# First attention: keys projected once and doubled by DMA. Second attention: logits as ring items, divisors moved by DMA, experts' weights split in its last batch

## The reference

```python
q = (x @ Mq).reshape(B, 8, 1024, 64)            # first attention; k alike
scores = einsum('bhqk,bhck->bhqc', q, k) / 8
att = softmax(scores, over the queries q)
out = einsum('bqhc,bhcd->bqhd', att as [B, C, H, C], v)
x = layernorm(x + out)

scores = einsum('bhst,...')                     # second: 16 heads, 4 of 8 channels, / 2
ao = softmax(scores) @ V                        # V has 4 channels a head
m = concat(ao, zeros) @ o_w + o_b
p = softmax(m @ router_w + router_b)            # 8 experts
keep the 2 largest of p, divided by their sum -> combine
moe = sum over e: combine[e] * (gelu(m @ w1[e] + b1[e]) @ w2[e] + b2[e])
x = layernorm(x + 0.3 * moe)
```

## Time and profile before

| | us |
|---|---|
| median of 3 runs | 1932.06 (1929.78 to 1940.83) |
| the profiled execution | 1930.25 |
| its span, first to last instruction | 1928.5 |
| first loads and values | 0 to 24.6 |
| first attention | 24.6 to 521.5 |
| layer norm, projections, first row maxima | 521.5 to 585.1 |
| second attention, blocks 0 to 30 | 585.1 to 1182.25 |
| its last block and its tail | 1182.25 to 1238.4 |
| routing | 1238.4 to 1263.7 |
| experts | 1263.7 to 1456.8 |
| state-space layer, sorted experts, gather | 1456.8 to 1928.5 |

### The profile page before, as it was taken

One profiled execution on the slowest core, in us unless ns is written; L12 is line 12 of the kernel. 1 busy time (PEld: TensorE's weight loads), 2 busy tenths in 40 slices (PEclk: granted clock), 3 DMA queues, 4 the chain that ended last, 5 costly groups with the idle time before them and its releaser, 6 DMA issues. The chain is left out here.

```text
span 1928.5 us, 39668 instructions
## 1 busy us (share of the span) xinstructions
PE 1630.0 (85%) x14336; PEld 901.3 (47%) x14337; DVE 1319.5 (68%) x1787; ACT 1274.3 (66%) x2303; POOL 476.2 (25%) x656
## 2 busy tenths in 40 slices
PE   5999999999979999999999999699997436704870
PEld 4555655555543443344444444377772112304860
DVE  2667677676679999999999994245554596341445
ACT  2777777777738898998989997378885760402221
POOL 0222222222162000000000000189991232042006
PEclk8999999999969999999999998599998768857995
DMA  5000000000013100110010000164300000412013
GB/s 203 2 0 0 0 0 0 0 0 0 1 36 99 28 16 2 23 24 1 16 28 5 2 1 1 44 148 97 93 17 14 1 0 0 151 34 77 23 30 84
DMA packets 42890, 62.64 MB, mean 32 GB/s; under 512 B 7768, under 2 KB 28000, under 8 KB 42016
## 3 DMA queue, kind: packets, MB, share of 16 engines
q1 hardware_dynamic: 38688, 55.97, 10.5%
q0 software_dynamic: 4096, 5.25, 1.0%
HBM read 34.85 MB, written 9.57 MB: 23 GB/s over the span
## 5 line engine op out<-in xcount | busy, mean ns | idle before, releaser
L862 ACT ACTIVATE m_probs<-m_ring 128x512 f32<-128x512 f32 x1024 | 545.8, 595 | 97.9 <-PE m_ring L776 81.5
L928 DVE TENSOR_REDUCE m_half_max<-m_pairs 128x2 f32<-128x1024 f32 x512 | 587.8, 1217 | 13.9 <-PE m_pairs L759 12.8
L351 DVE TENSOR_REDUCE a_neg_max<-a_scores 128x1 f32<-128x1024 f32 x257 | 310.5, 1215 | 118.6 <-PE a_scores L287 118.5
L341 ACT ACTIVATE a_probs<-a_scores,a_neg_max 128x1024 f32<-128x1024 f32 x256 | 285.3, 1114 | 127.2 <-DVE a_neg_max L351 127.2
L776 PE MATMUL m_ring<-m_q_max,m_k 32*128 32x512 f32 x1024 | 330.8, 505 | 5.8 <-DVE m_q_max L942 4.0
L791 PE MATMUL m_acc<-m_probs,m_v_aug 128*32 128x256 f32 (+1 forms) x4032 | 332.1, 403 | 0.0
L759 PE MATMUL m_pairs<-m_k,m_q 32*128 32x512 f32 x1024 | 263.3, 511 | 13.3 <-DVE m_half_max L928 9.6
L776 PEld LDWEIGHTS m_ring<-m_q_max,m_k 32*128 32x128 f32 x1024 | 152.4, 185 | 226.7 <-ACT m_probs L862 131.1
L287 PE MATMUL a_scores<-a_q,a_k 64*128 64x512 f32 x1032 | 257.2, 617 | 0.9 <-ACT a_probs L341 0.9
L386 POOL TENSOR_TENSOR a_scaled<-values,a_inv 128x128 f32<-128x128 f32 x256 | 102.7, 401 | 417.6 <-DVE a_inv L369 283.9
L1323 POOL TENSOR_TENSOR e_g_parts<-e_gated,e_g_parts 128x512 fp32r<-128x512 f32 x128 | 164.7, 1321 | 16.5 <-ACT e_g_parts L1269 15.6
(11 more groups left out here) (254 smaller groups left out, 1848.3 us busy)
## 6 DMA issues: line engine op xcount, KB each, us to landing
e_gates<-sorted_results SPq DMA_DIRECT2D x64, 256.0 KB, 3.7
m_k<-m_k_init SPq DMA_DIRECT2D x8, 512.0 KB, 8.8
m_q<-xT SPq DMA_DIRECT2D x8, 512.0 KB, 10.3
sorted_tokens<-xT SPq DMA_DIRECT2D x5, 512.0 KB, 6.0
f_sorted_rows<-sorted_tokens SPq DMA_DIRECT2D x10, 256.0 KB, 4.9
sorted_results<-f_out SPq DMA_DIRECT2D x10, 256.0 KB, 2.2
e_w<-e_w_dram SPq DMA_DIRECT2D x1, 2064.0 KB, 7.8
xT<-x_t_dram SPq DMA_DIRECT2D x1, 2048.0 KB, 7.6
```

Of the source, the lines that this page charges most:

```text
L341: nc.scalar.activation(probs[:, g, :], scores[:, slot(h * G + g), :], ACT.Exp, bias=neg_max[:, g:g + 1], accum_out=total[:, g:g + 1]).then ...
L351: nc.vector.tensor_reduce(neg_max[:, i % G:i % G + 1], scores[:, slot(i), :], AX, ALU.max, negate=True).then_inc(max_done, 1)
L862: nc.scalar.activation(probs[:, u % SLOTS, head, :], ring[:, bank, :], ACT.Exp, scale=0.5).then_inc(ring_taken, 1)
L928: nc.vector.tensor_reduce(half_max[:, pair // PAIRS % 2, at:at + 2], pairs[:, pair % 2, :, :], AX, ALU.max).then_inc(pair_taken, 1)
```

## The change

- First attention: the keys are projected once (4 matmuls instead of 8, `project_keys`), as pairs of neighbouring groups on the two halves. ScalarE copies them to `k_own`, and SyncE copies each half to the other half of `k_other` by two DMAs (`double`). `score` takes `k_own` or `k_other` by the parity of g. Projections stand in the steps g = 0 and 2, ScalarE's copies behind exponentials 2 and 4. The 13 loads go out one a head, behind the doubling.
- Second attention: numerators and divisors have rows of their own (each head's divisor is repeated on four rows, 16 above its numerator, by new layouts of `v_init`, `w_out` and `small`, not shown below). `finish`, `pick` and F go; four DMAs from GpSimd's queue (`bring_divisors`) take the divisors from `sums` to their numerators' rows, L waits for them, and L, X and the multiplication take all 128 rows. L and X stand both in unit 4 (after two and after four exponentials), O after unit 7, behind C.
- A `route` becomes a ring item R, after unit 2 of each block n % 4 == 3 from block 7 on, with a copy by ScalarE; block 31 has one of them. The eighth follows the tail. The bias is added in the routing stage.
- The experts' weights come as one input `e0_w`, in four pieces of 1024 columns, into `plain`, after the last spread of queries and keys; GpSimd splits one piece in each of the blocks 25 to 28 into the tiles of the even batches' queries and keys, which are kept for the experts' stage. The routing stage loads biases alone and splits no weights.
- Routing turns `ROWS_AHEAD` = 2 slices of gates; slices 2 to 7 are turned in the experts' stage, by TensorE after unit 10 of the chunk before (`turn_gates`), in the chunk's own bank of `acc`, copied by ScalarE after unit 11 and written by SyncE.
- `w_k` halves and `consts` loses `pick`.

```diff
-                for to, at in loads:
-                    sp.dma_start(to, at).then_inc(loaded, 16)
+                def double(head, p):
+                    sp.wait_ge(keys_copied, head + 1)
+                    for h in range(2):
+                        sp.dma_start(k_other[64 - 64 * h:128 - 64 * h, p, :, :],
...
+                double(0, 0)
+                for head in range(TILES):
+                    double(head + 1, (head + 1) % 2)
+                    if head < len(loads):
+                        to, at = loads[head]
+                        sp.dma_start(to, at).then_inc(loaded, 16)
+                sp.wait_ge(keys_doubled, DUP * (TILES + 1))
...
-                def project(head, c):
-                    pe.wait_ge(copied, COPIES * head + c)
...
+                def project_keys(head):
+                    pe.wait_ge(queries_copied, head)
                     for j in range(4):
-                        w = w_q[:, j, :] if c == 0 else w_k[:, 4 * (c - 1) + j, :]
-                        last = nc.tensor.matmul(proj[:, j * TILE:(j + 1) * TILE], w, xT[:, at], start=True, stop=True)
-                    last.then_inc(projected, 1)
+                        last = nc.tensor.matmul(proj[:, j * TILE:(j + 1) * TILE], w_k[:, j, :], xT[:, tokens(head)],
+                                                start=True, stop=True)
+                    last.then_inc(keys_projected, 1)
...
+                def project_queries(head):
+                    pe.wait_ge(keys_copied, head + 1)
...
                     if g == 0:
-                        pe.wait_ge(copied, COPIES * head + 2)
-                    if g == 4:
-                        pe.wait_ge(copied, COPIES * head + 3)
+                        pe.wait_ge(queries_copied, head + 1)
+                        pe.wait_ge(keys_doubled, DUP * head + DUP)
                     pe.wait_ge(exp_done, CREDIT + n - back(i) + 1)
                     for h in range(2):
                         rows = slice(64 * h, 64 * h + 64)
-                        last = nc.tensor.matmul(scores[:, slot(i), h * BANK:(h + 1) * BANK], k[rows, p, g, :],
+                        keys = k_own if g % 2 == h else k_other
+                        last = nc.tensor.matmul(scores[:, slot(i), h * BANK:(h + 1) * BANK], keys[rows, p, g // 2, :],
...
-                            if g < 2 * COPIES:
-                                project(head + 1, g // 2)
+                            if g == 0:
+                                project_keys(head + 1)
+                            if g == 2:
+                                project_queries(head + 1)
...
-                            if g in (3, 5, 7):
-                                copy(head + 1, (g - 3) // 2, (h + 1) % 2)
+                            if g == 2:
+                                copy_keys(head + 1, (h + 1) % 2)
+                            if g == 4:
+                                copy_queries(head + 1, (h + 1) % 2)
...
-                if last and (u, at % HG) in ((4, 2), (5, 0)):
-                    items.append(("LX"[u - 4], None, None))
+                if last and (u, at % HG) in ((4, 2), (4, 0)):
+                    items.append(("XL"[at % HG // 2], None, None))
...
-        if last and u in (1, 3, 6):
-            items.append(("S F  O"[u - 1], None, None))
+        if last and u == 1:
+            items.append(("S", None, None))
         if n in (1, 2) and u == 0 and number < BLOCKS_ALL - BLOCKS_OF:
             items.append(("P", n - 1, None))
+        if n % GROUPS == 3 and number > GROUPS and u == 2:
+            items.append(("R", None, None))
         if u == 6 and number + 1 < BLOCKS_ALL:
             items.append(("C", None, None))
+        if last and u == 7:
+            items.append(("O", None, None))
...
-        IN_RING = "EPCFO"
+        IN_RING = "EPCOR"
...
+                    for t in range(4):
+                        at = S + f * BANK + t * TILE
+                        last = nc.tensor.matmul(o[:, t * E:(t + 1) * E], mla[:, at:at + TILE], router[:, 0:E],
+                                                start=True, stop=True)
+                    last.then_inc(ring_full, 1)
...
-                            elif number == BLOCKS_ALL - 1 and which % 2 == 1 and which // 2 < BLOCKS_ALL // GROUPS - 1:
-                                route(which // 2)
...
                 def take_sums(f):
                     act.wait_ge(weighed, UNITS * GROUPS * (f + 1))
+                    if f >= 2:
+                        act.wait_ge(ao_done, f - 1)
                     nc.scalar.activation(sums[:, f % 2, :], acc[:, :], ACT.Copy).then_inc(sums_done, 1)
-                def take_heads(f, bank):
+                def logarithms(f):
+                    act.wait_ge(divisors_in, BROUGHT * (f + 1))
+                    nc.scalar.activation(log_sum[:, :], divisors[:, :], ACT.Ln).then_inc(log_done, 1)
...
+                def take_logits(f, bank):
+                    nc.scalar.activation(logits[:, 4 * f:4 * f + 4, :].rearrange("p t e -> p (t e)"),
+                                         ring[:, bank, 0:4 * E], ACT.Copy).then_inc(ring_taken, 1)
...
+                for n in range(PIECES):
+                    if n:
+                        sp.wait_ge(piece_done, n)
+                    sp.dma_start(plain[:, :, :].rearrange("p a n -> p (a n)"), weights[n]).then_inc(piece_in, 16)
...
+                def split_weights(n):
+                    whole = plain[:, :, :].rearrange("p a n -> p (a n)")
+                    pool.wait_ge(piece_in, 16 * (n + 1))
+                    if n == 0:
+                        pool.wait_ge(ring_taken, by_scalar(UNIT_AT[BLOCKS_ALL - BLOCKS_OF - 1, UNITS - 1]))
+                    nc.gpsimd.tensor_copy(piece(q[0], n), whole).then_inc(piece_hi, 1)
+                    pool.wait_ge(piece_hi, n + 1)
+                    nc.gpsimd.tensor_tensor(piece(k[0], n), whole, piece(q[0], n).bitcast(F32),
+                                            ALU.subtract).then_inc(piece_done, 1)
+                def bring_divisors(f):
+                    pool.wait_ge(sums_done, f + 1)
+                    if f:
+                        pool.wait_ge(log_done, f)
+                    for j in range(HG):
+                        pool.dma_start(divisors[32 * j:32 * j + 16, :],
+                                       sums[32 * j + 16:32 * j + 32, f % 2, :]).then_inc(divisors_in, 16)
                 def normalize(f):
...
                     if n % GROUPS == 0 and number:
+                        bring_divisors(number // GROUPS - 1)
                         normalize(number // GROUPS - 1)
+                    if 0 <= number - SPLIT_FROM < PIECES:
+                        split_weights(number - SPLIT_FROM)
...
-                for c in range(TILES // 4):
+                for c in range(ROWS_AHEAD):
...
-                pool.wait_ge(loaded, 16 * len(loads))
-                for n, (weights, hi, lo) in enumerate(to_split):
-                    if n == 1:
-                        pool.wait_ge(x_ready, 1)
-                        nc.gpsimd.tensor_tensor(x_parts[:, 1, 0, :], x_in[:, 0:BANK], x_parts[:, 0, 0, :].bitcast(F32),
-                                                ALU.subtract).then_inc(x_ready, 1)
-                    nc.gpsimd.tensor_copy(hi, weights).then_inc(hi_done, 1)
-                    pool.wait_ge(hi_done, n + 1)
-                    nc.gpsimd.tensor_tensor(lo, weights, hi.bitcast(F32), ALU.subtract).then_inc(lo_done, 1)
-                pool.wait_ge(lo_done, len(to_split))
+                pool.wait_ge(x_ready, 1)
+                nc.gpsimd.tensor_tensor(x_parts[:, 1, 0, :], x_in[:, 0:BANK], x_parts[:, 0, 0, :].bitcast(F32),
+                                        ALU.subtract).then_inc(x_ready, 1)
...
+                    if c >= ROWS_AHEAD:
+                        sp.wait_ge(rows_set, c - ROWS_AHEAD + 1)
+                        sp.dma_start(gate_dram[:, tokens_of(c)], rows[:, tokens_of(c)]).then_inc(written[c], 16)
...
                         pe.wait_ge(taken, c - 1)
+                        pe.wait_ge(rows_set, c - ROWS_AHEAD + 1)
...
+                def turn_gates(c):
+                    pe.wait_ge(taken, c - 1)
+                    for t in range(4):
+                        last = nc.tensor.matmul(acc[0:E, c % 2, t * TILE:(t + 1) * TILE], gate[:, 4 * c + t, :], ident,
+                                                start=True, stop=True)
+                    last.then_inc(turned, 1)
...
+                    if n % U == 10 and ROWS_AHEAD <= n // U + 1 < CH:
+                        turn_gates(n // U + 1)
...
+                def take_rows(c):
+                    act.wait_ge(turned, c - ROWS_AHEAD + 1)
+                    nc.scalar.activation(rows[:, tokens_of(c)], acc[0:E, c % 2, :], ACT.Copy).then_inc(rows_set, 1)
...
+                    if n % U == 11 and ROWS_AHEAD <= n // U + 1 < CH:
+                        take_rows(n // U + 1)
```

203 lines of the change are left out of this document (102 added, 101 removed).

## The result

The changed kernel takes 1877.1 us (median of 4, 1874.33 to 1880.14) against 1935.0 us before (median of 4 in the same comparison), a ratio of 0.970 with a 95% interval of 0.966 to 0.974. The profiled execution took 1874.33 us (span 1872.1) against 1930.25 (span 1928.5), 56 us less; 59.5 were forecast.

| stretch | before | after | difference | forecast |
|---|---|---|---|---|
| start, to the first score | 37.5 | 35.1 | -2.3 | -2.0 |
| first attention, first score to last mixing | 484.0 | 458.0 | -26.0 | -26.6 |
| norm, projections, first maxima | 52.1 | 52.2 | +0.1 | 0 |
| columns of block 0 to columns of block 31 | 608.8 | 605.7 | -3.1 | -6.2 |
| last block, its columns to its sums | 46.1 | 22.3 | -23.8 | -24.5 |

A forecast was written before the change was run, and what follows sets the result against it. TensorE was taken to bound the first attention and experts, VectorE the second attention's steps; its last block and the routing stage were bound otherwise. Terms summed to -59.5, so 1930.25 became 1871 us, range 1857 to 1889.

The forecast's parts named there:

- First attention: Each of 32 heads loses 1.09 us of projections, 34.9 in all; waits at 8 loop ends return 8: -26.6.
- Rival 2: First attention: exponentials, not TensorE, bound the short steps, so every head loses 1.0 us; 24 us more, 1895; chance 0.10.
- Rival 4: First attention: the keys' doubling lands late, 2.8 us a head, 88 us in all, 1959, slower than before; chance 0.03.
- Steady part: Second attention: 7 finishing blocks gain 1.23 each, leaving 1.25 of 2.48 for ScalarE's longer work; six R cost 2.4: -6.2.
- Last block: Second attention's last block, six of seven routings gone: full clock except a short fall after R, -24.5.
- rival 1: Second attention's last block stays at half clock: gain 14.8 in place of 24.5, 1881; chance 0.17.
- Tail: After the last sums, the divisors' DMAs, 4.3 us, stand before the logarithms: +2.4.
- Routing stage: GpSimd's weight-splitting chain gone, two gate slices turned instead of eight, 0.5 to the next stage: -7.9.
- Experts: Experts' stage: six gate slices turned where TensorE has no idle time, 0.88 us each: +5.3.
- Rival 5: GpSimd's splits beside VectorE block it, eight split instructions all colliding: +10, 1881; chance 0.04.
- Rival 3: Experts' stage: late gate rows or a fuller stage cost 2 us for each of 6 chunks, 1883; chance 0.08.
- Rival 6: Second attention's steady blocks: R lets the clock fall six times for a few us, +9, 1880; chance 0.05.

The follow-up runs named there:

- the mend: Changed kernel with all divisor transfers issued by SyncE instead of GpSimd, together with a three-head loop, later weight splits and the seventh routing in block 30: median 1862.8 us.

## Why the prediction was right, point by point

- **Start: right,** -2.3 against -2.0.
- **First attention: right.** The step of 2.93 twice in a row, the head of 13.89, the loss at a loop's end (1.10, I took 1.0) and no loss in a head. (The -26.6 itself is 26.9 by its terms; nothing stands for the 0.3.) Rival 2 is out: the exponentials wait for nobody inside a head. Rival 4 was placed rightly; one pair of transfers has room for a second.
- **Steady part: the sign right, the size half.** Gained 3.1 instead of 6.2, and the terms differ more than the sum. The finishing blocks gained 1.96 each where I had 1.23, the blocks behind them gave 0.43 back, which I didn't have; together 1.5. A routing costs 0.46 (I took 0.4). The failed step is the sentence that only block 28 has both a split and a finish, "already charged within the 1.25". It wasn't: 4.3 us, shown by moving the split. I had named the queue and not added it up: the split starts only after the reciprocals, so its 3.5 us lie ahead of the columns whole, which is 1.7 of the 4.3; the other 2.6 are the 6.8 us at half clock that followed, and these don't come in every execution.
- **Last block: right in the clock, with luck in the number.** 22.3 against a forecast of 21.7. Putting the routings back brings 43.5. But my sum at full clock, 20.2, counts 32 exponentials where the stretch has 36; with them it is 19.7 + 0.9 + 1.8 = 22.4, which is what was measured. The 2.2 us that I left out were made up for by the 1.5 that I allowed for a short fall of the clock, which didn't come in this execution. And rival 1 is alive in a milder form: with one routing left the clock still fell in three of seven traces, at a price of 6 to 8 us, so the seventh routing was the thing to move.
- **Tail: right in kind.** 4.2 us to the logarithm, 2.4 of loss forecast, 1.8 measured: from the end of the sums' copy the transfers took 3.6 us where I had 4.3.
- **Routing stage: mis-sized.** -6.2 instead of -7.9. The chain on VectorE took 11.3 us and the two turns 4.05, both within 0.1 of what I had. The term that I had at nothing is GpSimd's longer closing instruction: the stage began 2.6 us behind the last logits instead of 1.4, and the mend gave 1.4 back. The change to the next stage took 0.8 for my 0.5. No row of before showed it on the path, since there it ended in time.
- **Experts: mis-sized.** +6.7 instead of +5.3. I priced a slice by ScalarE's cadence, 0.88; on TensorE, which is what has no time there, it is eight records, 1.0 us busy, in chunks longer by 24.46 - 23.37 = 1.09, and 6 x 1.09 = 6.5.
- **The unchanged rest: luck.** It gave 3.7 us that nobody forecast. The same instructions took 467.9 to 475.5 us over all the traces, so that much of the agreement between 59.5 and 56 is scatter: without it the change is worth 52.7 by the stages.

Rival 5 didn't come in the blocks, where the splits stand beside maxima read from PSUM; it cost about 1 us in the routing stage, where a multiplication stood 1.37 us beside the token split. Rival 3 is out, since TensorE waits for no gate row. Rival 6 didn't come: in the changed kernel's trace the clock doesn't fall from 557.5 to block 28, where the six routings stand.

## What to carry to other kernels

Count what lies between two marks before pricing the stretch between them. Price a moved instruction on the engine that has no time where it goes, and write down for each in-order queue what stands behind it when it starts late, not only whether both fit. Where a stretch of TensorE runs at half clock without being idle, look at the matmuls between the others: moving the smallest ones elsewhere (46.1 to 22.3 us), and even adding a full one beside each (36.6), shortened the stretch here. A wait at a loop's end can be removed by the length of the loop, but a longer body has its own price at each return; choose the shorter length that fits.

## What the runs showed of the hardware that I had not expected

- A loop written out for six heads paid 8.2 to 8.8 us at each return, with 0.8 MB more brought by the instruction queue in the kernel; the loop of three heads paid nothing that can be seen (13.89 over its ends), that of four nothing but the 1.10 us of its wait. A head is 365 matmuls and weight loads of TensorE in the changed kernel's trace, so the bodies hold some 1100, 1460 and 2190 of them; where between the last two the price begins was not looked for.
- GpSimd's closing instruction of the second attention's stage took 5.30 us with 48 transfers issued by GpSimd in the stage, 7.59 with 76 and 7.92 with 80, however long ago they had landed.
- TensorE busy 42.6 of 42.9 us had the lower level for 37.5 of them, with seven routings among narrow matmuls; with one it kept the upper level for the whole block in four of seven traces, with none in both.
- The same instructions don't get the same clock in every execution: behind a stop of 1.6 us in block 28 the lower level held for 6.8, 3.4 or 0 us, and at the second attention's beginning for 37.5, 47.8 or 54.6.
